# Gathers and edge tiles of 127 rows in place of 128 in a graph and feed-forward layer on one core

## The chip, the cores and the metric

The kernel runs on one core of a Trainium2 chip. The metric is the device time of one execution in microseconds; lower is better. The kernel before takes 2657.89 us, the median of two runs (2651.34 and 2664.45).

## What is computed

The input is 6250 nodes with 256 float32 features and 206,250 directed edges, sorted by destination, each with one of 8 relations. The layer is

```python
hx = einsum('ni,rio->rno', layernorm(x), weight)          # 8 relations, 256 x 256
agg = segment_sum(hx[edge_type, src], dst, num_segments=6250)
x = x + agg * 0.5**0.5 + h_bias + (layernorm(x) @ loop_weight) * 0.5**0.5
z = layernorm(x)                                          # then, on the 3124 nodes with the largest z @ wr + br:
y = (gelu(z @ w1 + b1) @ w2 + b2) * (z @ wr + br)         # 256 -> 1024 -> 256
x = x + z + y                                             # y is 0 on the other nodes
```

## The kernel before

**Staging.** Nodes are cut into 49 blocks of 128 (`NB`). First the layer norm of all nodes is written to a table in device memory (`normed_table`), in seven chunks. Edges are cut into groups of `GE` = 4 x 128 = 512 consecutive ones (`J` = 4 tiles of `P` = 128). Edge lists lie in SBUF with one group per partition; TensorE turns them (L549) and ACT copies them out (L452), so that `gather_rows` and `keys` hold, for each group and tile, one number per partition: the source node, and destination minus the smallest destination of the half group plus 16 x relation.

**The loop.** Four groups make a round (`SLOTS` = 4), one for each message buffer. POOL issues for each group four gathers (L359): each takes 128 row numbers from `row_slots` and brings 128 rows of 1024 bytes from the table into the 128 partitions of `messages`. Before a slot's gathers POOL waits until the slot's sums of the round before are done (`pair_summed`), and before a round until ACT has refilled the row numbers (`rows_ready`, L510). VectorE builds one-hot matrices from the keys, for two slots at a time (L849). TensorE multiplies messages by one-hots, 8 float32 products per slot, each of which shows as two records (L611); this sums the rows that go to the same (relation, node) pair. VectorE adds the result to a window of `sums` (L931). There are 101 rounds: one ahead of the loop and 100 in it.

**Blocks.** When all edges of a block of 128 nodes are in, the block passes through three steps in three successive rounds. It *enters*: ACT closes and clears its half of `sums` (L477, L483), TensorE multiplies with the relation weights (L631) and the loop weights (L634). It *follows*: layer norm, transpose and first feed-forward product (L650), gelu on ACT (L498). It *leaves*: second product (L659). Which block does what in a round is worked out on the chip in `order_stage` from the destinations. A block enters in about every second round. TensorE's order in a round is written out: sums of slot 0, second product, sums of slot 1, turn of the loop input, sums of slot 2, turn of the feed-forward input, sums of slot 3, first product, relation products. Three drain rounds follow (`DRAIN`), and then the choice of the 3124 nodes and the output.

**Numbers that set the sizes** (L44 to L54): `NG_FULL` is the number of whole groups, 402; `NG` the number of groups rounded up to a whole number of rounds, 404, of which 403 hold edges; `ROUNDS` must be odd, because the loop on POOL treats the rounds in pairs. Padding groups gather row 0 and have keys that match no column. If a half group should span 16 or more nodes, or the block order be broken, a general path does the edges one by one instead (`general_load`, `general_gather`); with these inputs it isn't taken.

Of the kernel before, what the change touches and what calls it, by code (L numbers as in the profile page):

```python
# [23 lines left out]
P = 128  # L24
# [8 lines left out]
def gnn_ffn_program(nc, x, src, dst, edge_type, rel_w, h_bias, loop_w, wr, br, w1, b1, w2, b2, out):  # L33
    N, D = x.shape
    E = src.shape[0]
# [4 lines left out]
    NB = -(-N // P)  # L40
# [2 lines left out]
    NCH = NB // CH  # L43
    J = 4  # L44
    GP = 2
    GE = J * P
    SLOTS = 4
    NG_FULL = E // GE
    NG = -(-(-(-E // GE)) // SLOTS) * SLOTS
    NGT = NG + SLOTS  # L50
    ROUNDS = NG // SLOTS
    CONSTS = 7
    GT = 4
    W = P // R  # L54
# [14 lines left out]
    with ctx:  # L69
# [6 lines left out]
        table = nc.dram_tensor("normed_table", [NB * P, D], F32).ap()  # L76
# [5 lines left out]
        messages = sb("messages", [P, SLOTS, J * D])  # L82
# [32 lines left out]
        row_slots = sb("row_slots", [P, 2, SLOTS * J], I32)  # L115
# [17 lines left out]
        ident = sb("ident", [P, P])  # L133
        iota0 = sb("iota0", [P, P])
# [43 lines left out]
        banks = [ctx.enter_context(nc.psum_tensor(f"bank{i}", [P, BANK], F32)) for i in range(8)]  # L178
# [51 lines left out]
        general_in = sem("general_in")  # L230
# [10 lines left out]
        general_added = sem("general_added")  # L241
# [73 lines left out]
        def _(pool):  # L315
# [36 lines left out]
            def gather_round(i, half):  # L352
                pool.wait_ge(rows_ready, i + 1)
                for u in range(SLOTS):
                    if not isinstance(i, int):
                        pool.wait_ge(pair_summed[u], i)
                    pool.sem_inc(pool_carrier, 1)
                    for j in range(J):
                        pool.indirect_dma_start(messages[:, u, j * D:(j + 1) * D], None, table,  # L359
                                                bass.IndirectOffsetOnAxis(ap=row_slots[:, half, u * J + j:u * J + j + 1], axis=0),  # L360
                                                bounds_check=last_row).then_inc(gathered[u], 16)

            gather_round(0, 0)

# [3 lines left out]
            def general_load(g, whole):  # L370

                for to, a in ((edge_src, src), (edge_type_i, edge_type), (edge_dst, dst)):
                    for first, n, parts in (((0, J, P),) if whole else ((0, (E - g * GE) // P, P),
                                                                       ((E - g * GE) // P, 1, (E - g * GE) % P))):
                        if n == 0 or parts == 0:
                            continue
                        piece = a[0:NG_FULL * GE].rearrange("(g j p) -> g p j", p=P, j=J)[g] if whole else \
                            a[g * GE + first * P:g * GE + first * P + n * parts].rearrange("(j p) -> p j", p=parts)
                        pool.dma_start(to[0:parts, first:first + n], piece,
                                       allow_slow_non_contiguous=True).then_inc(general_in, 16)  # L380

# [7 lines left out]
            with pool.If(flag > 0):  # L389

                pool.sem_inc(general_added, 1)
                with pool.Fori(0, NG_FULL) as g:
                    pool.wait_ge(general_added, g * NB + 1)
                    pool.sem_inc(pool_carrier, 1)
                    general_load(g, True)
                    pool.wait_ge(general_in, 48 * (g + 1))
                    pool.sem_inc(pool_carrier, 1)
                    general_gather()

                pool.wait_ge(general_added, NG_FULL * NB + 1)  # L400
                nc.gpsimd.memset(edge_src[:, :], 0).then_inc(general_pads, 1)
                nc.gpsimd.memset(edge_type_i[:, :], 0).then_inc(general_pads, 1)
                nc.gpsimd.memset(edge_dst[:, :], -1).then_inc(general_pads, 1)
                pool.wait_ge(general_pads, 3)
                general_load(NG_FULL, False)
                pool.wait_ge(general_in, 48 * NG_FULL + 96)
                general_gather()
                pool.wait_ge(general_added, (NG_FULL + 1) * NB + 1)

            with pool.Fori(0, ROUNDS // 2) as k:  # L410
                gather_round(2 * k + 1, 1)
# [3 lines left out]
        def _(act):  # L415
# [29 lines left out]
            def take_tables():  # L445

                for n in range(2 * GT):
                    k, t = n // GT, n % GT
                    to = (gather_rows, keys)[k]
                    width = min(P, NGT - t * P)  # L450
                    act.wait_ge(slab_turned, n + 1)
                    nc.scalar.activation(to[:, t * P:t * P + width, :].rearrange("p g j -> p j g"),  # L452
                                         banks[n % 2][:, :].rearrange("p (j g) -> p j g", j=J)[:, :, 0:width],
                                         ACT.Copy).then_inc(slab_taken, 1)

            act.wait_ge(consts, CONSTS)
# [4 lines left out]
            take_tables()  # L461
            act.wait_ge(slab_taken, 2 * GT)
            for i in range(2):
                nc.scalar.activation(row_slots[:, i, :], gather_rows[:, i * SLOTS:(i + 1) * SLOTS, :].rearrange("p g j -> p (g j)"),
                                     ACT.Copy).then_inc(rows_ready, 1)
            with act.Fori(1, NCH // 2) as i:
                norm_chunk(2 * i, 0, i)
# [37 lines left out]
            def refill_rows(i):  # L505

                for u in range(SLOTS):
                    act.wait_ge(gathered[u], 64 * i)
                act.sem_inc(wait_carrier, 1)
                nc.scalar.activation(row_slots[:, bass.ds((i + 1) & 1, 1), :].rearrange("p h n -> p (h n)"),  # L510
                                     gather_rows[:, bass.ds(SLOTS * i + SLOTS, SLOTS), :].rearrange("p g j -> p (g j)"),
                                     ACT.Copy).then_inc(rows_ready, 1)

            def finish_round(i):
# [19 lines left out]
        def _(pe):  # L534
# [5 lines left out]
            def turn_tables(k):  # L540

                slab = (src_f, key_s)[k]
                pe.wait_ge((src_f_ready, keys_flat)[k], 1)
                for t in range(GT):
                    n = k * GT + t
                    if n > 1:
                        pe.wait_ge(slab_taken, n - 1)
                    for j in range(J):
                        last = nc.tensor.transpose(banks[n % 2][:, j * P:(j + 1) * P], slab[:, t, j * P:(j + 1) * P], ident[:, :])  # L549
                    last.then_inc(slab_turned, 1)  # L550

            turn_tables(0)
# [42 lines left out]
            flag = pe.value_load(flag_i[0:1, 0:1], min_val=0, max_val=1)  # L595
            with pe.If(flag > 0):
                pe.wait_ge(rel_in, 16 * KC)
                with pe.Fori(0, NG_FULL + 1) as g:
                    general_pair(g)

            def sum_pair(i, u):
                pe.wait_ge(onehot_ready[u // 2], i + 1)
                pe.wait_ge(gathered[u], 64 * (i + 1))
                if not isinstance(i, int):
                    pe.wait_ge(sum_taken[u], 2 * i)
                for h in range(GP):
                    for k in range(KC):
                        for e in range(J // GP):
                            j = h * (J // GP) + e  # L610
                            last = nc.tensor.matmul(banks[u][:, h * D + k * P:h * D + (k + 1) * P],  # L611
                                                    messages[:, u, j * D + k * P:j * D + (k + 1) * P], onehot[:, u, j, :],
                                                    start=(e == 0), stop=(e == J // GP - 1))
                last.then_inc(pair_summed[u], 1)

# [90 lines left out]
        def _(dve):  # L706
            V = nc.vector
# [137 lines left out]
            def build(i, half):  # L845

                at = slice(SLOTS * i + 2 * half, SLOTS * i + 2 * half + 2) if isinstance(i, int) else \
                    bass.ds(SLOTS * i + 2 * half, 2)
                V.tensor_tensor(onehot[:, 2 * half:2 * half + 2, :, :].rearrange("p u j c -> p (u j) c"),  # L849
                                iota0[:, :].unsqueeze(1).broadcast_to([P, 2 * J, P]),  # L850
                                keys[:, at, :].rearrange("p g j -> p (g j)").unsqueeze(2).broadcast_to([P, 2 * J, P]),
                                ALU.is_equal).then_inc(onehot_ready[half], 1)

            dve.wait_ge(slab_taken, 2 * GT)
# [5 lines left out]
            with dve.If(flag > 0):  # L860
# [40 lines left out]
                        V.scalar_tensor_tensor(nodes[:, b, :], banks[4][:, 0:D], SCALE, nodes[:, b, :],  # L901
                                               ALU.mult, ALU.add).then_inc(general_added, 1)

                with dve.Fori(0, NG_FULL + 1) as g:
                    general_pair(g)
                dve.wait_ge(general_added, (NG_FULL + 1) * NB + 1)

            def add_pair(i, u):
# [199 lines left out]
```

## Time and profile before

| | before |
|---|---|
| median of the runs | 2657.89 us |
| span of the profiled execution | 2726.1 us |
| TensorE matmul busy | 1928.1 us (71%) |
| VectorE busy | 949.5 us (35%) |
| ScalarE (ACT) busy | 662.0 us (24%) |
| GpSimd (POOL) busy | 1758.0 us (64%) |
| DMA, mean over the span | 90 GB/s |

The span is that of one execution taken by the hardware profiler, and longer than the runs without it. Busy time leaves out instructions that only compute registers, branch, wait or issue. In the rows, PE is TensorE's matmul, PEld its weight load, DVE is VectorE, ACT ScalarE, SP SyncE; L359 is line 359 of the kernel.

### The profile page before, as it was taken

To read this page: it belongs to the slowest core of one execution; us is meant where nothing else is said; L and a number is where in the kernel's file an instruction comes from. 1 tells how busy PE (TensorE), PEld (TensorE's weight loads), DVE (VectorE), ACT (ScalarE), POOL (GpSimd) and SP (SyncE) were. 2 spreads that over 40 slices of the span, in tenths; PEclk is the share of its full clock that TensorE was granted. 3 is DMA by queue.
4 is the path that set the end of the run, shared out by engine and by line. 5 is a ranking of instruction groups with operands and counts; after the bars stand their busy time and mean duration, and the time that the engine had idled before them with its cause. 6 is when DMAs were issued, how large, how long until landed. Compare 5 with 4: busy or idle time off the path is not lost.

```text
span 2726.1 us, 40701 instructions
## 1 busy us (share of the span) xinstructions
PE 1928.1 (71%) x10848; PEld 1705.0 (63%) x10849; DVE 949.5 (35%) x1937; ACT 662.0 (24%) x1005; POOL 1758.0 (64%) x1641
## 2 busy tenths in 40 slices
PE   1478776777777777777677777787867786777671
PEld 0367766666767666666566666666756675666571
DVE  6323333333333433333233332332333333333336
ACT  5022221122222231231222222222222221232130
POOL 2667767776776777666667676666776666666620
PEclk7668888878888888788878887888978788888785
DMA  7423333322333233322223222322332232223212
GB/s 248 132 82 90 87 89 91 88 87 83 87 88 90 85 90 88 89 83 82 83 84 91 85 87 78 88 86 81 90 89 78 83 89 82 84 81 89 83 35 95
DMA packets 105730, 245.07 MB, mean 90 GB/s; under 512 B 28465, under 2 KB 50975, under 8 KB 105715
## 3 DMA queue, kind: packets, MB, share of 16 engines
q0 software_dynamic: 79264, 218.32, 27.7%
q1 hardware_dynamic: 26451, 26.58, 3.1%
q8 instruction: 6, 0.10, 0.0%
q14 instruction: 9, 0.07, 0.0%
HBM read 231.96 MB, written 12.82 MB: 90 GB/s over the span
## 4 chain that ended last, share of the span: by engine, by line
PE 34%; another core or an unknown queue 24%; issue 18%; POOL 9%; DVE 6%; ACT 4%; DVEq 3%; DMA 1%; ACTq 1%; POOLq 0%
PE bank L611 14%; PE bank L631 9%; POOL messages L359 8%; PE bank L659 7%; ACT L498 2%; PE bank L650 1%; DVE sums L931 1%; ACT hidden L498 1%; DVEq L920 1%; PE bank L634 1%; DMA messages<-normed_table,row_slots 1%; DVEq L931 1%; PE bank L642 1%; ACT messages L433 0%
## 5 line engine op out<-in xcount | busy, mean ns | idle before, releaser
L359 POOL DMA_INDIRECT messages<-normed_table,row_slots x1616 | 1743.8, 1079 | 843.1 <-issue 493.1
L611 PE MATMUL bank<-onehot,messages 128*128 128x128 f32 x6464 | 977.4, 305 | 265.4 <-issue 234.3
L611 PEld LDWEIGHTS bank<-onehot,messages 128*128 128x128 f32 x6464 | 900.4, 216 | 330.2 <-issue 321.2
L931 DVE SCALAR_TENSOR_TENSOR sums<-bank,regular,sums 128x256 f32 x808 | 391.1, 484 | 1425.6 <-remote 923.6
L631 PE MATMUL bank<-rel_sb,closed 128*128 128x256 f32 x1568 | 404.7, 410 | 65.0 <-issue 62.8
L631 PEld LDWEIGHTS bank<-rel_sb,closed 128*128 128x128 f32 x1568 | 319.5, 207 | 138.3 <-issue 93.6
L659 PE MATMUL bank<-w_sb,hidden 128*128 128x256 f32 x784 | 262.6, 508 | 173.3 <-ACT hidden L498 158.3
L659 PEld LDWEIGHTS bank<-w_sb,hidden 128*128 128x128 f32 x784 | 201.9, 264 | 228.5 <-issue 187.2
L849 DVE TENSOR_TENSOR onehot<-iota,keys 128x1024 f32<-128x1024 f32 x203 | 249.2, 1227 | 146.7 <-issue 134.2
L650 PE MATMUL bank<-normed_t,w_sb 128*128 128x128 f32 x1568 | 233.6, 314 | 57.3 <-ACT normed_t L491 32.8
L650 PEld LDWEIGHTS bank<-normed_t,w_sb 128*128 128x128 f32 x1568 | 224.9, 230 | 68.7 <-issue 68.1
L498 ACT ACTIVATE hidden<-bank,b_col 128x128 f32<-128x128 f32 x392 | 106.4, 383 | 508.8 <-remote 425.1
L488 ACT ACTIVATE deviation<-moments,eps 128x1 f32<-128x1 f32 x49 | 14.4, 295 | 720.7 <-DVE moments L960 537.2
L510 ACT ACT_TABLE_LOAD x100 | 128.3, 1283 | 71.2 <-DMA messages<-normed_table,row_slots 69.6
L477 ACT ACTIVATE closed<-sums 128x2048 f32 x49 | 93.4, 1906 | 213.0 <-DVE sums L942 177.4
L483 ACT ACTIVATE sums<-zero 128x2304 f32 x49 | 103.6, 2114 | 0.0
L642 PE MATMUL bank<-ident,normed 128*128 128x128 f32 x98 | 24.9, 342 | 107.9 <-issue 73.5
L642 PEld LDWEIGHTS bank<-ident,normed 128*128 128x128 f32 x98 | 11.2, 158 | 116.8 <-issue 96.5
L488 ACT ACT_TABLE_LOAD x49 | 62.9, 1283 | 67.9 <-issue 67.5
L491 ACT ACTIVATE normed_t<-bank 128x256 f32<-128x256 f32 x49 | 18.8, 383 | 206.8 <-remote 157.7
L498 ACT ACT_TABLE_LOAD x49 | 62.9, 1283 | 0.9
L479 ACT ACTIVATE normed_x_t<-bank 128x256 f32<-128x256 f32 x49 | 18.7, 381 | 175.1 <-remote 87.5
(149 smaller groups left out, 546.4 us busy)
## 6 DMA issues: line engine op xcount, KB each, us to landing
messages<-normed_table,row_slots POOLq DMA_INDIRECT x1616
normed_table<-messages SPq DMA_DIRECT2D x7, 896.0 KB, 4.8
normed_x<-normed_table SPq DMA_DIRECT2D x49, 128.0 KB
node_out<-nodes SPq DMA_DIRECT2D x12, 512.0 KB
nodes<-in_x POOLq DMA_DIRECT2D x6, 896.0 KB, 8.9
rel_sb<-in_L_gnn_weight SPq DMA_DIRECT2D x2, 1024.0 KB, 7.1
w_sb<-in_L_ffn_w SPq DMA_DIRECT2D x2, 1024.0 KB
acc<-in_dst SPq DMA_DIRECT2D x1, 768.0 KB
```

What stands on the lines that cost most here:

```text
L359: pool.indirect_dma_start(messages[:, u, j * D:(j + 1) * D], None, table, bass.IndirectOffsetOnAxis(ap=row_slots[:, half, u * J + j:u * J ...
L477: nc.scalar.activation(closed[:, :, :], sums[:, :, bass.ds(slot, P)], ACT.Copy).then_inc(closed_ready, 1)
L483: nc.scalar.activation(sums[:, :, bass.ds(slot, OPEN)], zero[:, 0:1].unsqueeze(1).broadcast_to([P, KR, OPEN]), ACT.Copy).then_inc(slot_cle ...
L488: nc.scalar.activation(deviation[:, :], moments[:, 1:2], ACT.Sqrt, bias=eps[:, 0:1]).then_inc(ffn_deviation, 1)
L498: last = nc.scalar.activation(hidden[:, m, :], banks[5 + m // 4][:, m % 4 * P:(m % 4 + 1) * P], ACT.Gelu_apprx_tanh, bias=b1_col[:, m:m + 1])
L510: nc.scalar.activation(row_slots[:, bass.ds((i + 1) & 1, 1), :].rearrange("p h n -> p (h n)"), gather_rows[:, bass.ds(SLOTS * i + SLOTS, S ...
L611: last = nc.tensor.matmul(banks[u][:, h * D + k * P:h * D + (k + 1) * P], messages[:, u, j * D + k * P:j * D + (k + 1) * P], onehot[:, u, ...
L631: last = nc.tensor.matmul(banks[4][:, 0:D], closed[:, n, :], rel_sb[:, k, r * D:(r + 1) * D], start=(n == 0), stop=False)
L650: last = nc.tensor.matmul(banks[5 + m // 4][:, m % 4 * P:(m % 4 + 1) * P], w1_sb[:, k, m * P:(m + 1) * P], normed_t[:, k, :], start=(k == ...
L659: last = nc.tensor.matmul(banks[7][:, 0:D], hidden[:, m, :], w2_sb[:, m, :], start=(m == 0), stop=(m == HC - 1))
L849: V.tensor_tensor(onehot[:, 2 * half:2 * half + 2, :, :].rearrange("p u j c -> p (u j) c"), iota0[:, :].unsqueeze(1).broadcast_to([P, 2 * ...
L931: V.scalar_tensor_tensor(sums[:, :, bass.ds(to[h], W)], banks[u][:, h * D:(h + 1) * D].rearrange("p (n m) -> p n m", m=W), regular[:, 0:1] ...
```

## The change

Tiles of edges have 127 rows (`EP`) in place of 128, so a group has 508 edges. `EP` limits the partitions that a gather fills, the partitions of the copies of the tables, of the one-hots and of the sums, and the width of the transposes. The number of rounds comes from a new formula. The general path keeps tiles of 128 and has constants of its own (`WHOLE_PAIR`, `PAIRS_FULL`), which replace `GE` and `NG_FULL` there; those lines are left out here.

```diff
-    GE = J * P
+    EP = 127
+    GE = J * EP
+    WHOLE_PAIR = J * P
+    PAIRS_FULL = E // WHOLE_PAIR
     SLOTS = 4
     NG_FULL = E // GE
-    NG = -(-(-(-E // GE)) // SLOTS) * SLOTS
+    ROUNDS = -(-(-(-E // GE)) // SLOTS) // 2 * 2 + 1
+    NG = ROUNDS * SLOTS
     NGT = NG + SLOTS
-    ROUNDS = NG // SLOTS
...
-                        pool.indirect_dma_start(messages[:, u, j * D:(j + 1) * D], None, table,
-                                                bass.IndirectOffsetOnAxis(ap=row_slots[:, half, u * J + j:u * J + j + 1], axis=0),
+                        pool.indirect_dma_start(messages[0:EP, u, j * D:(j + 1) * D], None, table,
+                                                bass.IndirectOffsetOnAxis(ap=row_slots[0:EP, half, u * J + j:u * J + j + 1], axis=0),
                                                 bounds_check=last_row).then_inc(gathered[u], 16)
...
-                    nc.scalar.activation(to[:, t * P:t * P + width, :].rearrange("p g j -> p j g"),
-                                         banks[n % 2][:, :].rearrange("p (j g) -> p j g", j=J)[:, :, 0:width],
+                    nc.scalar.activation(to[0:EP, t * P:t * P + width, :].rearrange("p g j -> p j g"),
+                                         banks[n % 2][0:EP, :].rearrange("p (j g) -> p j g", j=J)[:, :, 0:width],
...
-                nc.scalar.activation(row_slots[:, bass.ds((i + 1) & 1, 1), :].rearrange("p h n -> p (h n)"),
-                                     gather_rows[:, bass.ds(SLOTS * i + SLOTS, SLOTS), :].rearrange("p g j -> p (g j)"),
+                nc.scalar.activation(row_slots[0:EP, bass.ds((i + 1) & 1, 1), :].rearrange("p h n -> p (h n)"),
+                                     gather_rows[0:EP, bass.ds(SLOTS * i + SLOTS, SLOTS), :].rearrange("p g j -> p (g j)"),
...
-                        last = nc.tensor.transpose(banks[n % 2][:, j * P:(j + 1) * P], slab[:, t, j * P:(j + 1) * P], ident[:, :])
+                        last = nc.tensor.transpose(banks[n % 2][0:EP, j * P:(j + 1) * P], slab[:, t, j * EP:(j + 1) * EP], ident[:, :])
...
-                                                    messages[:, u, j * D + k * P:j * D + (k + 1) * P], onehot[:, u, j, :],
+                                                    messages[0:EP, u, j * D + k * P:j * D + (k + 1) * P], onehot[0:EP, u, j, :],
...
-                V.tensor_tensor(onehot[:, 2 * half:2 * half + 2, :, :].rearrange("p u j c -> p (u j) c"),
-                                iota0[:, :].unsqueeze(1).broadcast_to([P, 2 * J, P]),
-                                keys[:, at, :].rearrange("p g j -> p (g j)").unsqueeze(2).broadcast_to([P, 2 * J, P]),
+                V.tensor_tensor(onehot[0:EP, 2 * half:2 * half + 2, :, :].rearrange("p u j c -> p (u j) c"),
+                                iota0[0:EP, :].unsqueeze(1).broadcast_to([EP, 2 * J, P]),
+                                keys[0:EP, at, :].rearrange("p g j -> p (g j)").unsqueeze(2).broadcast_to([EP, 2 * J, P]),
                                 ALU.is_equal).then_inc(onehot_ready[half], 1)
```

## Rows read from the trace of the kernel before

**Rows 1.** The page's first part: busy time, share of the span, instructions.
```profile
PE 1928.1 (71%) x10848; PEld 1705.0 (63%) x10849; DVE 949.5 (35%) x1937; ACT 662.0 (24%) x1005; POOL 1758.0 (64%) x1641
```

**Rows 2.** Line 359 in the loop: stretch, POOL busy (x), granted clock, DMA share, GB/s.
```profile
97.57:2618.40 2520.83, 1726.39 (x1600) 0.82 0.30 86
```

**Rows 3.** The same stretch, POOL by line: busy, mean ns | idle before.
```profile
L359 POOL DMA_INDIRECT messages<-normed_table,row_slots x1600 | 1726.4, 1079 | 794.7 <-issue 488.8 <-remote 163.5 <-ACT row_slots L510 95.9
```

**Rows 4.** The same stretch, POOL's waits: us in total, times, longest.
```profile
POOL messages L359 <- issue: 488.8, 1448, 2.9
POOL messages L359 <- remote: 163.5, 92, 3.2
POOL messages L359 <- ACT row_slots L510: 95.9, 23, 6.2
POOL messages L359 <- PE bank L611: 46.4, 37, 4.8
```

**Rows 5.** POOL in order of time, round 1 (start, us, ..., idle before and releaser).
```profile
97.57 1.01 POOL L359 DMA_INDIRECT messages<-normed_table,row_slots  x1 [0.30 <-issue]
98.89 1.01 POOL L359 DMA_INDIRECT messages<-normed_table,row_slots  x1 [0.30 <-issue]
...
116.31 1.01 POOL L359 DMA_INDIRECT messages<-normed_table,row_slots  x1 [3.25 <-remote]
...
121.57 1.01 POOL L359 DMA_INDIRECT messages<-normed_table,row_slots  x1 [0.31 <-issue]
```

**Rows 6.** POOL in order of time, rounds 54 and 55.
```profile
1440.48 1.01 POOL L359 DMA_INDIRECT messages<-normed_table,row_slots  x1 [0.30 <-issue]
...
1447.06 2.02 POOL L359 DMA_INDIRECT messages<-normed_table,row_slots  x1 [0.30 <-issue]
...
1455.14 1.01 POOL L359 DMA_INDIRECT messages<-normed_table,row_slots  x1 [2.11 <-remote]
...
1464.39 1.01 POOL L359 DMA_INDIRECT messages<-normed_table,row_slots  x1 [0.30 <-issue]
```

**Rows 7.** PE and DVE in order of time, the same stretch.
```profile
1443.32 3.45 PE L611 MATMUL bank<-onehot,messages 128*128 128x128 f32 x16 [3.16 <-issue]
...
1446.97 1.23 DVE L849 TENSOR_TENSOR onehot<-iota,keys 128x1024 f32<-128x1024 f32 x1
```

**Rows 8.** Line 611: duration ns min/median/max, first and last start.
```profile
L611 PE MATMUL bank<-onehot,messages x6464: 269/275/582, 83.9 to 2625.3; 128*128 128x128 f32 x196
```

**Rows 9.** DVE in order of time, before the loop.
```profile
22.60 1.75 DVE L760 TENSOR_REDUCE hidden<-acc 128x6 f32<-128x1536 int32 x1
24.39 0.69 DVE L761 TENSOR_REDUCE hidden<-acc 128x2 f32<-128x512 f32 x1
...
34.07 2.29 DVE L766 SCALAR_TENSOR_TENSOR acc<-acc 128x2048 f32<-128x2048 int32 x1
```

**Rows 10.** Stretches: length, busy us of engines, granted clock, DMA share, GB/s.
```profile
35.00:35.60 0.60, 0.00 (x0) 0.00 (x0) 0.60 (x1) 0.00 (x0) 0.00 (x0) 0.50 0.68 227
36.20:36.50 0.30, 0.08 (x1) 0.08 (x2) 0.27 (x3) 0.00 (x0) 0.00 (x0) 0.50 0.06 21
2722.90:2725.30 2.40, 0.00 (x0) 0.00 (x0) 0.00 (x0) 0.00 (x0) 0.00 (x0) 0.50 0.13 42
```

**Rows 11.** DMA: POOL's queue (packets, MB, share of 16 engines) and two issues.
```profile
q0 software_dynamic: 79264, 218.32, 27.7%
...
nodes<-in_x POOLq DMA_DIRECT2D x1, 768.0 KB, 9.9
...
nodes<-in_x POOLq DMA_DIRECT2D x1, 106.0 KB, 10.1
```

**Rows 12.** POOL's plain loads: 896 rows (L342), 768 (L343), 106 (L345).
```profile
25.17 0.94 POOL L342 DMA_DIRECT2D nodes<-in_x  x1 [1.80 <-DMA nodes<-in_x]
26.10 0.84 POOL L343 DMA_DIRECT2D nodes<-in_x  x1
26.94 0.59 POOL L345 DMA_DIRECT2D nodes<-in_x  x1
```

More of the change, by code:

```diff
@@ L372, in general_load @@
                 for to, a in ((edge_src, src), (edge_type_i, edge_type), (edge_dst, dst)):
-                    for first, n, parts in (((0, J, P),) if whole else ((0, (E - g * GE) // P, P),
-                                                                       ((E - g * GE) // P, 1, (E - g * GE) % P))):
+                    for first, n, parts in (((0, J, P),) if whole else ((0, (E - g * WHOLE_PAIR) // P, P),
+                                                                       ((E - g * WHOLE_PAIR) // P, 1, (E - g * WHOLE_PAIR) % P))):
                         if n == 0 or parts == 0:
                             continue
-                        piece = a[0:NG_FULL * GE].rearrange("(g j p) -> g p j", p=P, j=J)[g] if whole else \
-                            a[g * GE + first * P:g * GE + first * P + n * parts].rearrange("(j p) -> p j", p=parts)
+                        piece = a[0:PAIRS_FULL * WHOLE_PAIR].rearrange("(g j p) -> g p j", p=P, j=J)[g] if whole else \
+                            a[g * WHOLE_PAIR + first * P:g * WHOLE_PAIR + first * P + n * parts].rearrange("(j p) -> p j", p=parts)
                         pool.dma_start(to[0:parts, first:first + n], piece,
@@ L391, in _ @@
                 pool.sem_inc(general_added, 1)
-                with pool.Fori(0, NG_FULL) as g:
+                with pool.Fori(0, PAIRS_FULL) as g:
                     pool.wait_ge(general_added, g * NB + 1)
@@ L398, in _ @@
                     general_gather()
-                pool.wait_ge(general_added, NG_FULL * NB + 1)
+                pool.wait_ge(general_added, PAIRS_FULL * NB + 1)
                 nc.gpsimd.memset(edge_src[:, :], 0).then_inc(general_pads, 1)
@@ L404, in _ @@
                 pool.wait_ge(general_pads, 3)
-                general_load(NG_FULL, False)
-                pool.wait_ge(general_in, 48 * NG_FULL + 96)
+                general_load(PAIRS_FULL, False)
+                pool.wait_ge(general_in, 48 * PAIRS_FULL + 96)
                 general_gather()
-                pool.wait_ge(general_added, (NG_FULL + 1) * NB + 1)
+                pool.wait_ge(general_added, (PAIRS_FULL + 1) * NB + 1)
             with pool.Fori(0, ROUNDS // 2) as k:
@@ L463, in _ @@
             for i in range(2):
-                nc.scalar.activation(row_slots[:, i, :], gather_rows[:, i * SLOTS:(i + 1) * SLOTS, :].rearrange("p g j -> p (g j)"),
+                nc.scalar.activation(row_slots[0:EP, i, :], gather_rows[0:EP, i * SLOTS:(i + 1) * SLOTS, :].rearrange("p g j -> p (g j)"),
                                      ACT.Copy).then_inc(rows_ready, 1)
@@ L597, in _ @@
                 pe.wait_ge(rel_in, 16 * KC)
-                with pe.Fori(0, NG_FULL + 1) as g:
+                with pe.Fori(0, PAIRS_FULL + 1) as g:
                     general_pair(g)
@@ L902, in general_pair @@
                                                ALU.mult, ALU.add).then_inc(general_added, 1)
-                with dve.Fori(0, NG_FULL + 1) as g:
+                with dve.Fori(0, PAIRS_FULL + 1) as g:
                     general_pair(g)
-                dve.wait_ge(general_added, (NG_FULL + 1) * NB + 1)
+                dve.wait_ge(general_added, (PAIRS_FULL + 1) * NB + 1)
             def add_pair(i, u):
```

## The prediction

> **What bounds the kernel now.** I read the page's engine shares first, then the main loop in one stretch, then POOL's waits in it, then single rounds. No engine is full: PE is busy 71% and POOL 64% of the span [rows 1]. The loop of 100 rounds from 97.57 to 2618.4 us is 2520.8 of the 2726.1 us, 25.2 us a round [rows 2]. POOL's 64% misleads. Between two gathers it always spends another 0.30 us that counts as idle, so a gather takes 1.01 + 0.30 = 1.316 us from start to start [rows 5], and 16 of them 21.06 us. The mean gather is 1.079 us, not 1.01 [rows 3]: some last up to 2.0 us, those that coincide with the DVE's one-hot build (the gather at 1447.06 beside the build at 1446.97) [rows 6, 7]. That is 16 x 0.067 = 1.07 us a round. So POOL's own work is 22.1 us of the 25.2. What is left, 3.1 us a round, is waiting: 794.7 us idle in the loop less 1600 x 0.30 = 480 leaves 315 us, released by PE, by ACT's refill of the row numbers, or by "remote", which at L359 is mostly PE's signal that a slot is summed [rows 3, 4].
>
> One round shows how the ring closes. The last gather of slot 3 starts at 1440.48. PE, idle for 3.16 us, starts that slot's sums at 1443.32, that is 2.84 us after the issue: the latency of a gather as PE sees it. POOL waits for slot 2 to be released until 1455.14, issues 8 gathers, and the last gather of the next round starts at 1464.39, 23.9 us after the first [rows 6, 7]. So one gather latency, one PE stretch and eight issues are in series in such a round, while POOL's own 22.1 us runs close behind. Both rings matter: more issue time and more latency each lengthen the round.
>
> **The change part by part.** A group is 4 x 127 = 508 edges in place of 512. 206,250 edges are 406 whole groups and 2 edges, 407 groups in place of 403. The new formula for the rounds gives 102 // 2 x 2 + 1 = 103 (an odd number is needed), so 412 groups are gathered in place of 404: 1648 gathers in place of 1616; the last round is padding altogether. What it adds:
>
> 1. Two rounds. POOL's floor for a round is 22.1 us; the average one is 25.2. The 49 blocks and their products (L631, L650, L659) don't grow, so the two rounds are light ones. The nearest row is round 1, before any block is entered: its first gather starts at 97.57, the next round's at 121.57, 24.0 us with one wait of 3.25 us [rows 5]. Bounds 22.1 and 25.2, I take 23.5: **+47 us** (44 to 50).
> 2. A gather carries 127 rows. Bytes fall by 0.8%. If the rows stay spread over the 16 engines, seven or eight on each, its latency stays; POOL's 1.01 us is for preparing it. I take no change, but this term is the whole question. Bounds: a gain of 1/128 of 1.01 us, 8 ns x 1648 = 13 us at most; the losses are rivals A and B.
> 3. Sums over 127 rows (L611), one-hots on 127 partitions (L849), copies of tables (L452, L464, L510). A matmul's length goes by its columns, which stay 128: 0.275 us by the median for all 6464 [rows 8]; the one-hot's 1024 elements per partition stay too. No change in each; the two rounds bring 128 more matmul records and 4 more builds, which lie inside term 1.
> 4. Before the loop: loads of edges with rows of 2032 bytes in place of 2048, transposes of 127 columns, reductions over 254 in place of 256 elements, the rest of 22 rows in place of 18. About 1% of pieces of 0.7 to 2.3 us [rows 9], and the gathers are released there by the table's stores, not by the indices: +-1 us.
> 5. After the loop: the last block enters in the first drain step, as before (worked out from the destinations: step 101 of 101 rounds, now step 103 of 103). The same tail. The spans of the half groups stay below 16 nodes and the block order holds, so the general path isn't taken.
>
> The sum is 2726.1 + 47 = 2773 us in a profiled execution. That execution took 68 us more than the median of the runs, 2657.9; the two rounds are worth 47 x 2657.9 / 2726.1 = 46 in it: **2704 us**, +1.7%.
>
> How rows are spread over engines is not shown for a gather of 127 rows. Two rows show it for another ragged count. SP's store of the 106 rows of the last block is alone at 2722.9 to 2725.3 us: the DMA engines are busy 0.13 of the time, which is two of sixteen, at 42 GB/s, 21 for each [rows 10]. POOL's load of the same 106 rows was issued 0.84 us after one of 768 KB, and they landed 10.1 and 9.9 us after their issues, so the small one came 1.0 us behind [rows 11, 12]; on two engines its 53 KiB each would have moved for 2.6 us, and in the stretch up to 35.6 us the engines were 0.68 busy at 227 GB/s and nearly idle from 36.2 on [rows 10]. So a store by SP falls back to few engines and a plain load by POOL does not. The gathers are POOL's, which is why I lean to "spread". The Trainium skill, DMA: Bandwidth & Descriptors, section "Why a DMA increments its semaphore by 16 and not by 1", states that the number of engines is the largest up to 16 that divides the row counts, and gives 1 for 127; it makes an exception for some direct copies by POOL. Both agree with it, and by its general rule a gather of 127 rows would sit on one engine, which is rival A.
>
> **Rivals.**
> A. *One engine for a whole gather*, the engines taking turns. At the 21 GB/s of an engine in the store [rows 10] 127 KiB take 6.2 us. From above: the packets of POOL's queue took 27.7% of 16 engines over the span for 218.32 MB [rows 11], 7.25 us of engine time for a gather. Spread it is a sixteenth, 0.45 us, so the latency grows by 5.7 to 6.8 us. A gather every 1.32 us over 16 engines leaves each engine 21 us for it, so no queue forms. But the latency is in series once a round [rows 6]: 103 x 5.7 to 6.8 = 590 to 700 us; if a fifth of the rounds hide it behind POOL's own order, 470. With the 46: 3170 to 3400, middle 3300 us. For it: SP's store. Against: POOL's load. This is the rival that ends on the other side (slower by 24%); it decides from a latency about 1 us longer.
> B. *POOL takes longer to prepare a ragged count.* Its loads took 0.84 us for 768 rows and 0.94 us for 896, 0.10 for the last 128; by that line 106 rows would be 0.32 us, but they took 0.59 [rows 12]: 0.27 us too much. In a gather that is 16 x 0.27 = 4.3 us a round. If it takes the place of the waits, only the part over the 3.1 us counts, 1.2 x 103 = 124; in full, 445. With the 46: 2830 to 3150, middle 2990 us.
> C. *POOL gets cheaper*, because one engine's descriptors are easier to write than sixteen's. The 106-row load's 0.59 against 0.84 [rows 12] is the nearest row: 0.25 x 1616 = 400 us of issue, of which the PE ring gives back perhaps half: 2500 us. Nothing else speaks for it.
>
> **How the numbers follow.** My forecast (spread, same issue time) 0.57; A 0.27; B 0.11; C 0.03; else 0.02. 2% of 2657.9 is 53 us, about what a measurement of this kernel can tell from no change, so the boundary is 2711. The forecast's own range is 2690 to 2720 and about a fifth of it lies above the boundary: within 2% 0.46; slower 0.11 + 0.27 + 0.11 + 0.02 = 0.51; faster 0.03. Slower is a little likelier than the single likeliest case, because the forecast sits just under the boundary. The range has to reach into A: 2690 to 3310 leaves out A's upper half, C and a little more, 0.2 in all.
>
> **What would show it.** Gathers x1648, last one 2617 + 47. Spread: PE's matmul at L611 starts 2.8 us after a slot's last issue, the DMA queue of POOL has about 49 packets a gather, the main loop takes 102 rounds of 25.1 us, and POOL's waits stay at 3 us a round. A: PE starts 8.5 to 9.6 us after the issue, gathers still last 1.01 us, POOL's waits grow to 8 us or more a round, under "remote" and PE, and the round to 30 or 31 us. B: the gather's median is above 1.01 us. I am also wrong if the two rounds cost less than 44 us, or if the time is far above 3400, which would mean that all single-engine gathers share one engine.

## The result and the profile after

The kernel after took 5068.34 us (median of 2 runs, 5065.84 to 5070.84), against 2657.89 before: 1.909 times as long, 95% interval 1.897 to 1.922. The forecast was 2704, and the range ended at 3310. The loss is larger than that of every rival in the prediction.

The page of the kernel after: the first part (busy us, share of the span, instructions), the clock row, the DMA queues (packets, MB, share of 16 engines), the chain of work that ended last, and the costliest group (busy us, mean ns | idle before and its releaser).

```profile
span 5064.1 us, 41218 instructions
...
PE 2279.0 (45%) x10976; PEld 2091.7 (41%) x10977; DVE 1009.5 (20%) x1957; ACT 667.6 (13%) x1009; POOL 4394.9 (87%) x1673
...
PEclk6666676666666766666766766676666766666766
...
DMA packets 898324, 260.13 MB, mean 51 GB/s; under 512 B 820026, under 2 KB 843751, under 8 KB 898309
...
q0 software_dynamic: 871840, 233.38, 24.4%
...
POOL 80%; issue 17%; DVE 1%; PE 1%; ACT 1%; DMA 1%; POOLq 0%; DVEq 0%; ACTq 0%
...
L362 POOL DMA_INDIRECT messages<-normed_table,row_slots x1648 | 4380.8, 2658 | 546.2 <-issue 546.2
```

Against [rows 1] POOL went from 64% to 87% of a span that nearly doubled, and the chain that ended last is POOL's gathers and the pauses between them, 97% in all. A gather has a mean of 2.658 us in place of 1.079 [rows 3], and no wait for another engine is left among its releasers, where 315 us of such waits stood before [rows 4]. Everything else only waits: PE has 351 us more busy time than before, at a granted clock of 0.674 in place of 0.81. That is a consequence, not a cause; PE is idle 55% of the span.

The source view of the gather's line (duration in ns: least, median, most; first and last start) and the landings:

```profile
L362 POOL DMA_INDIRECT messages<-normed_table,row_slots x1648: 2617/2621/3671, 74.4 to 4954.5; - x184
...
who waited for it (us, times):
  ACT L513: 1136.4, 54
  PE bank L614: 268.9, 64
...
DMA to landing us min/median/max: 8.0/8.1/11.4
```

The least and the median agree, so every gather is slow, not some. The very first one, for which nothing from POOL's gathers was outstanding yet, took 3.08 us, so the length is no wait for earlier gathers to drain:

```profile
74.40 3.08 POOL L362 DMA_INDIRECT messages<-normed_table,row_slots  x1 [44.19 <-issue]
```

The timeline of POOL and PE around one slot, which answers to [rows 6, 7] (start, us, engine, line, ..., idle before and releaser):

```profile
2509.49 2.62 POOL L362 DMA_INDIRECT messages<-normed_table,row_slots  x1 [0.30 <-issue]
...
2512.42 2.62 POOL L362 DMA_INDIRECT messages<-normed_table,row_slots  x1 [0.30 <-issue]
2515.34 2.62 POOL L362 DMA_INDIRECT messages<-normed_table,row_slots  x1 [0.30 <-issue]
...
2522.70 3.60 PE L614 MATMUL bank<-onehot,messages 127*128 127x128 f32 x16 [8.74 <-issue]
```

The gather of 2512.42 is the last of a slot's four (number 824 in order), and PE starts that slot's sums 10.28 us after it, against 2.84 before. Two things grew: POOL's part, 1.01 to 2.62 us, and what follows it, 1.83 to 7.66 us. POOL never waits for the second: it goes on at 2515.34 as if nothing were outstanding. By the landing times in the trace the first three gathers of a slot land 8.1 us after their start and the fourth 10.4 us (medians), and PE starts 0.09 us behind the fourth. The four count on one semaphore (`gathered[u]`), so the count for one gather can be filled by increments of the next; that the fourth shows the full latency is a reading that fits and was not tested.

**The books.** By the means of the pages the span grew by 5064.1 - 2726.1 = 2338.0 us. Gathers cost 1616 x (2.658 - 1.079) = 2552 us more and the 32 new ones 32 x 2.658 = 85; the new ones bring 32 x 0.30 = 10 us of pauses; the waits of 315 us [rows 3, 4] are gone. 2552 + 85 + 10 - 315 = 2332, which leaves 6 us. So the question is why a gather of 127 rows costs POOL 2.62 us.

### The profile page after: what moved, and what is told of

Its sections match the earlier page's. It is cut to its first block, busy times and chain, and to the rows that moved or that the text cites. A ratio compares the mean times of both kernels' runs of the same rounds, so it can differ in the third digit from the quotient of the medians.

```text
span 5064.1 us, 41218 instructions
## 1 busy us (share of the span) xinstructions
PE 2279.0 (45%) x10976; PEld 2091.7 (41%) x10977; DVE 1009.5 (20%) x1957; ACT 667.6 (13%) x1009; POOL 4394.9 (87%) x1673
## 2 busy tenths in 40 slices
DMA packets 898324, 260.13 MB, mean 51 GB/s; under 512 B 820026, under 2 KB 843751, under 8 KB 898309
## 4 chain that ended last, share of the span: by engine, by line
POOL 80%; issue 17%; DVE 1%; PE 1%; ACT 1%; DMA 1%; POOLq 0%; DVEq 0%; ACTq 0%
POOL messages L362 80%; PE bank L614 0%; ACT messages L436 0%; DMA messages<-normed_table,row_slots 0%; PE bank L634 0%; DVE nodes L1082 0%; DMA nodes<-in_x 0%; DVE messages L1046 0%; DVE messages L1048 0%; PE bank L662 0%; DMA normed_table<-messages 0%; PE bank L653 0%; PE bank L702 0%; POOLq L413 0%; DVE hidden L731 0%
## 5 line engine op out<-in xcount | busy, mean ns | idle before, releaser
L362 POOL DMA_INDIRECT messages<-normed_table,row_slots x1648 | 4380.8, 2658 | 546.2 <-issue 546.2
L614 PE MATMUL bank<-onehot,messages 127*128 127x128 f32 x6592 | 1419.5, 403 | 2648.4 <-issue 2379.2
L614 PEld LDWEIGHTS bank<-onehot,messages 127*128 127x128 f32 x6592 | 1325.4, 307 | 2752.6 <-issue 2750.8
L634 PE MATMUL bank<-rel_sb,closed 128*128 128x256 f32 x1568 | 375.8, 401 | 7.1 <-ACT normed_x_t L482 7.1
L852 DVE TENSOR_TENSOR onehot<-iota,keys 127x1024 f32<-127x1024 f32 x207 | 253.2, 1223 | 141.0 <-issue 129.4
L653 PE MATMUL bank<-normed_t,w_sb 128*128 128x128 f32 x1568 | 211.6, 300 | 0.6 <-ACT normed_t L494 0.6
L662 PE MATMUL bank<-w_sb,hidden 128*128 128x256 f32 x784 | 209.1, 427 | 2.4 <-ACT hidden L501 2.4
L662 PEld LDWEIGHTS bank<-w_sb,hidden 128*128 128x128 f32 x784 | 172.0, 226 | 29.1 <-issue 2.5
L983 DVE TENSOR_SCALAR acc<-acc,w_all x49 | 57.2, 1167 | 7.3
L637 PE MATMUL bank<-loop_sb,normed_x_t 128*128 128x256 f32 x196 | 50.3, 379 | 0.0
```

Of the source, the lines that this page charges most:

```text
L362: pool.indirect_dma_start(messages[0:EP, u, j * D:(j + 1) * D], None, table, bass.IndirectOffsetOnAxis(ap=row_slots[0:EP, half, u * J + j: ...
L634: last = nc.tensor.matmul(banks[4][:, 0:D], closed[:, n, :], rel_sb[:, k, r * D:(r + 1) * D], start=(n == 0), stop=False)
L653: last = nc.tensor.matmul(banks[5 + m // 4][:, m % 4 * P:(m % 4 + 1) * P], w1_sb[:, k, m * P:(m + 1) * P], normed_t[:, k, :], start=(k == ...
L662: last = nc.tensor.matmul(banks[7][:, 0:D], hidden[:, m, :], w2_sb[:, m, :], start=(m == 0), stop=(m == HC - 1))
L852: V.tensor_tensor(onehot[0:EP, 2 * half:2 * half + 2, :, :].rearrange("p u j c -> p (u j) c"), iota0[0:EP, :].unsqueeze(1).broadcast_to([E ...
```

## The experiments

They ran on three chips: on the first two the kernel before took 2399.14 and 2396.04 us (granted clock 0.87), on the third 2661.76 us (0.83), about as in the first pair of runs. g127, g126 and g124 belong to the chip with 2399.14 us, g125, g120, g112 and g31 to the one with 2396.04; each of these seven is a single run. Seven runs of the kernel before on the first chip lie between 2393.83 and 2401.95 us.

### Only the gathers, and all but the gathers

First the change was cut in two. g127 is the kernel before with nothing but the gathers cut to 127 rows. It leaves work out: the last row of each tile keeps what it held. (Half of one message buffer is cleared once before the loop, left out here.)

```diff
-pool.indirect_dma_start(messages[:, u, j * D:(j + 1) * D], None, table,
-                        bass.IndirectOffsetOnAxis(ap=row_slots[:, half, u * J + j:u * J + j + 1], axis=0),
+pool.indirect_dma_start(messages[0:127, u, j * D:(j + 1) * D], None, table,
+                        bass.IndirectOffsetOnAxis(ap=row_slots[0:127, half, u * J + j:u * J + j + 1], axis=0),
```

> Leaves work out: the kernel before (101 rounds of 128-row tiles), but each gather fetches only the first 127 of its 128 rows; the last row of each tile is left stale, everything else is as before. tiny packets per gather, a round 47 us, time about 2658 + 101 x 22.1 - a little = 4960 us. Theory R (the compute on 127 partitions, the table copies or the new round count carry part of the loss): clearly under 4900 us, with the gather nearer 1 us.

Measured: 4969.68 us against 2399.14. Its gathers, by the source view:

```profile
L360 POOL DMA_INDIRECT messages<-normed_table,row_slots x1616: 2613/2618/3618, 75.0 to 4854.7; - x180
...
DMA to landing us min/median/max: 8.0/8.1/11.6
```

fix128 is the complement: the kernel after with everything it brings (127-row tiles, 412 groups, 103 rounds), but each gather again over 128 partitions, the last row number being 0:

```diff
+nc.gpsimd.memset(row_slots[:, :, :], 0).then_inc(consts, 1)
...
-pool.indirect_dma_start(messages[0:EP, u, j * D:(j + 1) * D], None, table,
-                        bass.IndirectOffsetOnAxis(ap=row_slots[0:EP, half, u * J + j:u * J + j + 1], axis=0),
+pool.indirect_dma_start(messages[:, u, j * D:(j + 1) * D], None, table,
+                        bass.IndirectOffsetOnAxis(ap=row_slots[:, half, u * J + j:u * J + j + 1], axis=0),
```

> The changed kernel with one part undone: gathers fetch 128 rows again (the row number of partition 127 is 0), tiles, sums, one-hots, tables and the 103 rounds stay at 127. Theory T: the gather is back at 1.01 us and the time at 2658 + 44 to 50 = 2702 to 2708 us, ratio 1.017 to 1.019. Theory R: well above 2750 us.

Measured: 2447.36 us against 2399.14, ratio 1.021 (1.019 to 1.023), that is +48 us. The source view:

```profile
L363 POOL DMA_INDIRECT messages<-normed_table,row_slots x1648: 1007/1012/2040, 74.1 to 2332.2; - x184
```

POOL's largest group:

```profile
L363 POOL DMA_INDIRECT messages<-normed_table,row_slots x1648 | 1756.9, 1066 | 546.0 <-issue 471.7 <-DMA normed_table<-messages 43.8 <-PE bank L615 29.3
```

One row back in the gather takes the median from 2.62 to 1.01 us and the time to within 48 us of before. The whole loss beyond the two rounds is in the gather's form. The +48 is the size of the prediction's term 1 (+47), met on a chip where POOL hardly waits (its 546.0 us of idle time are 1648 pauses of 0.30 us, the 43.8 us before the first gather, and 8 us more): there POOL's own time for 32 gathers, 32 x (1.066 + 0.30) = 44 us, makes nearly all of it.

### Which property of 127

127 is odd, prime, and not full. g126, g124, g125, g120 and g112 are g127 with 126, 124, 125, 120 and 112 in place of 127. All five leave work out in the same way: the rows of a tile that are not fetched keep what they held.

> Leaves work out: the kernel before with gathers of 126 rows; the last two rows of each tile are left stale. 126 = 14 x 9. Theory T: 14 engines carry 9 rows each, 16 x 9 = 144 descriptors, 1.01 + 16 x 0.00085 = 1.02 us on POOL, a time within 1% of 2658 us. Theory F (any count that is not a multiple of 16 takes POOL's slow path): 2.6 us and about 4960 us.

> Leaves work out: the kernel before with gathers of 124 rows; the last four rows of each tile are left stale. 124 = 4 x 31. Theory T: 4 engines carry 31 rows each, 16 x 31 = 496 descriptors; with (2.62 - 1.01) us over (2032 - 128) descriptors = 0.85 ns each it is 1.01 + 0.31 = 1.32 us on POOL; landing about 1.5 us later than with 128. 16 x 1.62 = 26 us a round is over the present 25.2, so POOL is the bound and the time is 2658 + 101 x 1 to 3 = 2760 to 2960 us. Theory F: 2.6 us and about 4960 us.

> Leaves work out: the kernel before with gathers of 125 rows (the last three rows of each tile stale). 125 = 5 x 25, and 5 does not divide the table's 6272 rows. POOL's times so far are 1.01 us for 8 rows per engine (128), 1.09 for 9 (126), 1.39 for 31 (124), 2.62 for 127 (127): beyond 8, 0.97 us + 0.0128 us per row on the fullest engine. Theory T1 (the engines are the largest divisor up to 16 of the gather's own row count): 5 engines with 25 rows, 0.97 + 0.32 = 1.31 us, time 1616 x (1.31 + 0.30 + about 0.04) + 190 = 2860 us. Theory T2 (the divisor must divide the table's rows too): one engine, 2.6 us, about 4940 us. Theory F (each step away from 128 costs more): between 1.09 and 1.39 us, without the packets telling 25 rows.

> Leaves work out: the kernel before with gathers of 120 rows (8 rows of each tile stale). T1: 15 engines with 8 rows, 0.97 + 0.10 = 1.07 us, time about 2490 us. T2: 8 engines with 15 rows, 1.16 us, about 2630 us. Theory F (distance from 128): above 1.39 us, since 120 is further from 128 than 124.

> Leaves work out: the kernel before with gathers of 112 rows (16 rows of each tile stale). T: all 16 engines with 7 rows; if the 16-engine case has a path of its own that saves the 0.06 us by which 8 rows on 16 engines lie under the line through 9, 31 and 127, POOL takes 1.00 us, and the time is 2370 to 2400 us, no more than before on this chip. Theory F: more than 1.39 us.

What each showed: time, then POOL's gather (median and mean in us), the packets of one gather by size in bytes, and "k", the largest number up to 16 that divides the rows. The packets are those of POOL's queue in the trace, less the 1696 of its plain loads before the first gather; they come out whole.

| rows | k x rows on each | time, us | median | mean | packets | of 4096, 3072 or 1024 | of 16 or 12 | of 4 |
|---|---|---|---|---|---|---|---|---|
| 128 (fix128) | 16 x 8 | 2447.36 | 1.012 | 1.066 | 48 | 32 | 0 | 16 |
| 112 | 16 x 7 | 2388.67 | 1.002 | 1.063 | 48 | 32 | 0 | 16 |
| 120 | 15 x 8 | 2511.51 | 1.096 | 1.137 | 48 | 30 | 2 | 16 |
| 126 | 14 x 9 | 2509.53 | 1.086 | 1.135 | 64 | 42 | 4 | 18 |
| 125 | 5 x 25 | 2806.27 | 1.287 | 1.320 | 128 | 35 | 66 | 27 |
| 124 | 4 x 31 | 2954.41 | 1.393 | 1.412 | 144 | 32 | 96 | 16 |
| 127 (g127) | 1 x 127 | 4969.68 | 2.618 | 2.655 | 528 | 32 | 480 | 16 |

(128 has 1648 gathers, the others 1616.) The times are POOL's: the idle time before gathers is 535 to 537 us in all runs with 1616 gathers here, so only the mean of a gather differs. (The 7 us by which 112 rows are under the kernel before are no more than what two runs of one kernel differ by.) From 128 rows to 124 it gives 1616 x (1.412 - 1.066) = 559 us, and 555 were measured; to 127 it gives 2568, and 2571 were measured. The queue's row in g125 and in g124, loads included (packets, MB, share of 16 engines):

```profile
q0 software_dynamic: 208544, 215.13, 31.1%
```

```profile
q0 software_dynamic: 234400, 214.10, 29.4%
```

The Trainium skill, DMA: Bandwidth & Descriptors, section "Why a DMA increments its semaphore by 16 and not by 1", gives the divisor rule; by it k is 1 for 127, and the packets agree.

The expectations had the placement right in all five runs and POOL's time only roughly. g126 was to cost 1.02 us a gather and less than 1% of the time; it cost 1.086 us and 110 us, 4.6%. g124 was to take 1.32 us and took 1.393, g120 1.07 and took 1.096, g125 1.31 and took 1.287. Theory F failed: neither does every count that 16 doesn't divide cost 2.6 us, nor does the cost grow with the distance from 128.

### Bytes or rows

g31 gathers 31 rows: k is 1, the list is 31 long as in g124, but it carries a quarter of the bytes.

> Leaves work out: the kernel before with gathers of only 31 rows, a quarter of the bytes (97 rows of each tile stale). 31 is prime: one engine with 31 rows. T: POOL's time goes by the rows on the fullest engine, not by the rows gathered: 1.39 us as with 124 rows on four engines, and about the time of that run, 2954 us, with a quarter of the data. A theory by which bytes, or the number of rows that POOL looks up, set the time: well under 1.0 us and a time of 2400 us or less, PE's own work being the bound.

Measured: 2906.04 us. The source view:

```profile
L360 POOL DMA_INDIRECT messages<-normed_table,row_slots x1616: 1333/1337/2387, 75.4 to 2796.0; - x180
...
DMA to landing us min/median/max: 3.8/4.1/6.4
```

POOL's queue:

```profile
q0 software_dynamic: 234400, 60.81, 11.9%
```

60.81 MB in place of 214.10, and the gather takes 1.337 us against 1.393. A quarter of the rows and nearly the same cost: POOL's time goes with the length of the longest list, hardly with rows or bytes. With one engine in use both times, 127 against 31 rows, 96 rows more on the list cost 2.618 - 1.337 = 1.281 us: 13.3 ns for each row of the list, or, as an estimate, 0.83 ns for each of the 16 entries (a row and fifteen dummies) that it adds. From 8 to 31 rows, 15 and 4 engines, it is (1.393 - 1.096) / 23 = 12.9 ns. That is an average, not a law: from 8 to 25 rows it is 11 ns, from 25 to 31 18 ns, and 9 rows on 14 engines cost 0.010 us less than 8 on 15. The step from 16 engines to 15 at 8 rows costs 0.08 us by itself (1.012 to 1.096).

That POOL writes the dummies entry by entry is the reading that fits; it is argued, not shown. g31 and g124 both have 16 lists of 31, with 465 and 372 dummies among the entries, and g31, where 93 rows are replaced by dummies, is 0.056 us cheaper. But the sum of all entries was 16 times the longest list in every run, so a price per entry and a price per step of the longest list aren't told apart.

### Latency alone

Rival A had the placement right and priced it by latency. late keeps the 128-row gathers and makes PE wait, before it sums a slot, for the next slot's gathers too, so that PE gets each slot four gathers later at the same cost to POOL:

```diff
+if u < SLOTS - 1:
+    pe.wait_ge(gathered[u + 1], 64 * (i + 1))
+elif not isinstance(i, int) or i < ROUNDS - 1:
+    pe.wait_ge(gathered[0], 64 * (i + 2))
```

The last round is taken out of PE's loop for it, since no gathers follow it.

> The kernel before with 128-row gathers; before PE sums slot u it also waits until the next slot's four gathers have landed. To PE each slot so seems to land four gathers, about 5.3 us, later, which is the latency that the 127-row gather added (8.1 against 2.8 us from issue); POOL's price of a gather is unchanged. Theory L (latency is in series once a round, as the prediction has it): 101 x 5.3 = +535 us, about 2930 us. Theory H (four slots of buffers hide it, and POOL's own time decides): the slots come back 5.3 us later but POOL needs them only 3 slots later, 15 us; 2400 to 2500 us, POOL's waits grow by less than 100 us.

again is the kernel before, unchanged. Its expectation, like late's, was written for a chip where that kernel takes 2399 us; both ran on the one where it takes 2661.76.

> The kernel before, unchanged, for its profile on the chip of the experiments (there it took 2399 us, clock 0.87). If POOL sets the pace there: gather median about 1.01 us, mean about 1.06, POOL's waits in the loop well under the 315 us of the first trace, span about 2400 us. If the ring through PE still sets it: waits of 200 us or more.

Measured: late 2669.32 us against 2661.76, ratio 1.0033 (1.0007 to 1.0059): +8 us. again 2651.31 us. The edit did what it says: PE waits 464.6 us for gathers before its sums, against 19.6 in again. The source view of the gather's line in late, then in again (who waited for it, us, times):

```profile
  PE bank L615: 464.6, 198
```

```profile
  PE bank L611: 19.6, 9
```

In late's timeline the gather at 1298.23 is the last of slot 0, and PE sums slot 0 at 1306.53, 8.3 us later, once slot 1's last gather (1303.48) has landed:

```profile
1298.23 1.01 POOL L359 DMA_INDIRECT messages<-normed_table,row_slots  x1 [0.31 <-issue]
...
1303.48 1.01 POOL L359 DMA_INDIRECT messages<-normed_table,row_slots  x1 [0.30 <-issue]
1306.53 2.49 PE L615 MATMUL bank<-onehot,messages 128*128 128x128 f32 x16 [1.81 <-DMA messages<-normed_table,row_slots]
1306.67 1.01 POOL L359 DMA_INDIRECT messages<-normed_table,row_slots  x1 [2.17 <-remote]
```

POOL's group in again, then in late:

```profile
L359 POOL DMA_INDIRECT messages<-normed_table,row_slots x1616 | 1746.4, 1081 | 767.3 <-issue 473.9 <-remote 179.1 <-ACT row_slots L510 52.0
```

```profile
L359 POOL DMA_INDIRECT messages<-normed_table,row_slots x1616 | 1735.3, 1074 | 788.5 <-issue 482.8 <-remote 198.4 <-ACT row_slots L510 44.1
```

PE sums a slot four gathers later, some 5.3 us (5.5 in the slot shown, 8.3 against 2.8), and POOL's idle time grows by 21 us in all, not by 535. The waits of POOL before are not a ring through a gather's latency; the four slots take up the latency in between.

The trace before says so too. Round 54 sums slot 2 from 1438.14 to 1440.16:

```profile
1438.14 2.02 PE L611 MATMUL bank<-onehot,messages 128*128 128x128 f32 x16 [0.82 <-issue]
```

POOL goes on with that slot only at 1455.14 [rows 6], 15 us later. It can't have waited for those sums. The same holds for all 77 first gathers of a slot that the trace puts down to "remote": their slot had been summed 2.4 us before or earlier. What held POOL there stays open. The chain that ended last gives "another core or an unknown queue" 24% in the kernel before, 20, 15 and 24% in again, late and split2, and nothing in fix128 and the seven g runs, on chips where the kernel before takes 10% less; it has nothing in the kernel after either.

Two limits of late. It adds less latency than the 127-row gather did (10.28 - 2.84 = 7.4 us; its expectation took 8.1 us, the median landing, where a slot's fourth gather has 10.4), and it takes one slot of the four for it, so the price of the other 2 us stays open. And its granted clock was a little higher, 0.846 against 0.831 in again, with 34 us less PE busy time; part of the latency's price may hide behind that, though far from 535 us. In the kernel after the latency costs nothing, since POOL waits for no one.

### A build that leaves POOL alone

The gather's mean lies 0.067 us above its median, which the prediction put down to the DVE's one-hot build. split2 is the kernel before with that build in short one-input comparisons:

```diff
-V.tensor_tensor(onehot[:, 2 * half:2 * half + 2, :, :].rearrange("p u j c -> p (u j) c"),
...
+V.tensor_copy(keyf[:, half, :].rearrange("p (g j) -> p g j", j=J), keys[:, at, :]).then_inc(keys_cast, 1)
+dve.wait_ge(keys_cast, 2 * i + half + 1)
+for v in range(2):
+    for j in range(J):
+        last = V.tensor_scalar(onehot[:, 2 * half + v, j, :], iota0[:, :],
+                               keyf[:, half, v * J + j:v * J + j + 1], None, ALU.is_equal)
```

> The kernel before with the one-hot build split: instead of one two-input comparison over 1024 elements, a cast of 8 keys and 8 one-input comparisons of 128 elements against one key per partition. If the gather's mean lies 0.05 to 0.07 us above its median because POOL waits for the DVE's long two-input instruction, then mean falls to the median, 1616 x 0.05 = 80 us less where POOL sets the pace: about 2320 us. If the gathers are slow beside any DVE work, or the DVE's 8 short instructions cost more than they free: 2400 or above.

Measured: 2791.71 us against 2661.76, ratio 1.051 (1.045 to 1.057), slower. POOL's group and the DVE's two:

```profile
L361 POOL DMA_INDIRECT messages<-normed_table,row_slots x1616 | 1657.7, 1026 | 989.0 <-issue 495.5 <-ACT row_slots L512 194.2 <-remote 161.2
...
L857 DVE TENSOR_SCALAR onehot<-iota,keyf 128x128 f32<-128x128 f32 x1624 | 346.1, 304 | 12.3 <-issue 3.1 <-DVE keyf L853 2.4
L853 DVE CAST keyf<-keys 128x8 f32 (+1 forms) x203 | 36.4, 179 | 161.1 <-issue 149.1 <-ACT sums L485 11.8 <-DVE flag_i L843 0.2
```

Half of the theory holds: the mean falls from 1.081 to 1.026 us, 89 us less for POOL, while the median stays (1.012 and 1.015), so the long two-input build was what held gathers up. The other half fails. POOL's idle time rises by 989.0 - 767.3 = 222 us, and 222 - 89 = 133 of the span's 138 us. The DVE now spends 346.1 + 36.4 = 382 us on the build against 249. POOL's waits grew at the refill of the row numbers by ACT (52 to 194 us) and at PE's sums (18.5 to 94.2). The granted clock was also lower, 0.806 against 0.831. Which of these comes first isn't settled. No version here that does all the work beats the kernel before.

## Why the prediction was wrong, point by point

- *What bounds the kernel.* POOL's pace of 1.316 us and the 0.067 us of collisions were read rightly (split2 takes most of the latter away). "Remote" as mostly PE's signal that a slot is summed was misread: the slot of 1455.14 had been summed 15 us before. With it goes "one gather latency, one PE stretch and eight issues are in series": late shows +8 us for some 5.3 us more of latency in every slot.
- *Term 1, two rounds, +47:* right in size; fix128 has +48. It ran on the chip without the 3.1 us of waits a round, where by the prediction's own floor 2 x 22.1 = 44 would be due, so part of the agreement is luck.
- *Term 2, "a gather carries 127 rows ... I take no change":* this is the step that failed. The rows don't stay spread; they sit on one engine, and POOL's time for a gather, taken as unchanged at a mean of 1.079 us, rose to 2.658. That is 1616 x 1.579 = 2552 us which the sum had at nothing. The text called it the whole question and then decided it by POOL's plain load of 106 rows, which stayed close behind its neighbour. As far as these rows tell, a plain load and a gather from the same queue don't share the placement, and nothing in the trace had shown a ragged gather. The row of SP's store, two engines for 106 rows, was the one that carried over.
- *Terms 3 to 5:* nothing contradicts them. fix128 holds all three inside its +48; none was measured by itself.
- *Rival A, one engine:* right in the placement and in the size of the latency (forecast 5.7 to 6.8 us; 7.66 - 1.83 = 5.8 behind POOL's part; 7.4 from the start), wrong in both things that made its time. It said "gathers still last 1.01 us"; they last 2.62. And it multiplied the latency by 103 rounds, 590 to 700 us, where late shows 8 for 5.3 us of it. The "about 49 packets a gather" of the forecast (48 and a share of the loads) against the 528 measured is the sign by which the placement could be told apart.
- *Rival B, POOL takes longer:* the right mechanism for the time, sized six times too small: 0.27 us, again from the 106-row load, where the mean rose by 1.58. Its own sum with that number comes out: 16 x 1.58 = 25.3 us a round, less the 3.1 of waits, times 103 rounds, and the 47 of term 1 make 2334, against 2338 measured in the profiled executions. A and B were priced as alternatives. They are one: the placement on one engine comes with the long lists and with POOL's longer time, in every run here.
- *Rival C, POOL cheaper with one engine:* false, of the opposite sign.
- *"Far above 3400 ... all single-engine gathers share one engine":* the time is far above 3400, and they don't. A gather of 127 KiB every 2.93 us is 44 GB/s, twice the 21 GB/s of one engine in SP's store, and the last gathers land no later than the first. The sign missed its own rival B, which also ends there once the price is 1.58 us.
- *The range:* it ended where A's latency ended. With the unknown price of a ragged gather bounded only by a row of 0.27 us, the upper end had no ground; the prediction's own remark that no trace row showed such a gather was the reason to leave more above 3310.

## What to carry to other kernels

Keep a gather's row count a multiple of 16, and pad it with a harmless row number rather than cut a row: g127 differs from the kernel before in one row of 128 and took 4970 us in place of 2399. Where a transfer is placed on fewer engines, look at what the issuing engine pays for it before the transfer's latency. Before pricing a latency as "in series", ask how many buffers lie between the two engines, and look up when the awaited work in fact ended; here four slots hid over 5 us of latency, and a wait that looked like PE's was not for PE's sums.

## What the runs showed of the hardware

- POOL's time for a gather grows by some 13 ns on average for each row on the fullest engine's list, from 1.01 us (8 rows, 16 engines) to 2.62 us (127, one engine), and hardly depends on bytes (1.337 and 1.393 us for 31 and 124 rows).
- Engines that carry no row of a gather still get lists as long as the one that does: 528 packets in place of 48, of which 480 are of 16 or 12 bytes.
- The number of engines of a gather follows its own row count (125 rows: 5, beside a table of 6272).
- The pause of 0.30 us between two gathers is the same at every size.
- With 127-row gathers the first three of a slot land after 8.1 us and the fourth after 10.4, and PE starts 0.09 us behind the fourth; why they differ wasn't tested.
- The kernel before takes 2396 to 2399 us on two chips and 2642 to 2676 on a third, with POOL waits under "remote" on the third; what they are wasn't settled.
